# A ring of three PSUM banks for the first products of an expert layer, with two kinds of transposes sharing one bank

## The reference

```python
x = x + conv(_ln_c(x))            # attention over 256 positions, 8 images of 64 channels
t = _to_tokens(x)                 # 2048 tokens of 64 channels
t = t + ffn(_ln_t(t))
# ffn: the router picks 2 of 8 experts for each token, gates sum to 1
h1 = jnp.einsum('nc,ehc->neh', flat, w1)      # 64 -> 682
h3 = jnp.einsum('nc,ehc->neh', flat, w3)      # 64 -> 682
h = jax.nn.silu(h1) * h3
y = jnp.einsum('neh,ech->nec', h, w2)         # 682 -> 64
out = jnp.einsum('ne,nec->nc', gates, y)
```

## Time and profile before

| | |
|---|---|
| median of 3 runs | 235.94 us (235.25 to 236.06) |
| profiled execution, its own time | 233.65 us |
| its span | 231.9 us |
| mean granted TensorE clock | 0.826 of full speed |
| TensorE matmul busy | 156.4 us (67%) |
| TensorE weight load busy | 135.8 us (59%) |
| VectorE busy | 109.8 us (47%) |
| GpSimd busy | 85.7 us (37%) |
| ScalarE busy | 72.1 us (31%) |
| HBM traffic | 143 GB/s over the span |

### The profile page before, as it was taken

One profiled execution on the slowest core, in us unless ns is written; L12 is line 12 of the kernel. 1 busy time (PEld: TensorE's weight loads), 2 busy tenths in 40 slices (PEclk: granted clock), 3 DMA queues, 4 the chain that ended last, 5 costly groups with the idle time before them and its releaser, 6 DMA issues.

```text
span 231.9 us, 4952 instructions
## 1 busy us (share of the span) xinstructions
PE 156.4 (67%) x1714; PEld 135.8 (59%) x1714; DVE 109.8 (47%) x398; ACT 72.1 (31%) x154; POOL 85.7 (37%) x109
## 2 busy tenths in 40 slices
PE   2647898698924000049988888888888889898031
PEld 2527896687813000048977777777777777786010
DVE  2696598679457700014544444444444444442050
ACT  2236445341000000024533444444444444432011
POOL 6142520206777777600033333333333333336400
PEclk9999999655555555557999999999999999999655
DMA  4999600000101000020276766677677766500053
GB/s 136 429 390 420 285 0 3 0 0 7 31 18 33 23 29 23 29 47 15 91 269 219 252 231 236 224 240 246 222 233 233 244 220 201 168 11 20 23 181 91
DMA packets 16314, 33.47 MB, mean 144 GB/s; under 512 B 7826, under 2 KB 9010, under 8 KB 15778
## 3 DMA queue, kind: packets, MB, share of 16 engines
q1 hardware_dynamic: 14018, 30.80, 38.8%
q0 software_dynamic: 2272, 2.36, 3.1%
HBM read 25.94 MB, written 7.21 MB: 143 GB/s over the span
## 4 chain that ended last, share of the span: by engine, by line
issue 40%; POOL 29%; DVE 9%; PE 9%; DMA 5%; ACT 3%; POOLq 1%; SPq 0%; ACTq 0%
POOL ys L335 15%; POOL xs L294 13%; PE bank L803 2%; DVE xn L477 2%; PE bank L791 2%; DMA y_in<-ys 2%; DVE kq_right L509 1%; POOL rstd L278 1%; DVE neg_max L514 1%; DMA x_sb<-x_tok 1%; PE bank L769 1%; PE bank L753 1%; DMA xs<-rows,pos 1%; DMA ys<-y_out,y_row 1%; ACT probs L367 1%
## 5 line engine op out<-in xcount | busy, mean ns | idle before, releaser
L917 PE MATMUL bank<-x_cols,weights 64*128 64x128 f32 x468 | 64.2, 287 | 10.3 <-ACT act_sb L429 9.3
L713 DVE TENSOR_TENSOR hid<-bank,act_sb 128x512 f32<-128x512 f32 (+1 forms) x60 | 40.5, 676 | 62.2 <-ACT act_sb L429 60.5
L335 POOL DMA_INDIRECT ys<-y_out,y_row x39 | 37.3, 957 | 83.7 <-DVE y_out L721 77.1
L917 PEld LDWEIGHTS bank<-x_cols,weights 64*128 64x128 f32 x468 | 57.3, 194 | 17.1 <-ACT act_sb L429 12.3
L919 PE MATMUL bank<-x_cols,weights 64*128 64x128 f32 x468 | 64.2, 287 | 0.0
L919 PEld LDWEIGHTS bank<-x_cols,weights 64*128 64x128 f32 x468 | 57.3, 194 | 0.0
L429 ACT ACTIVATE act_sb<-bank 128x512 f32<-128x512 f32 (+1 forms) x60 | 35.1, 586 | 43.6 <-PE bank L917 43.5
L294 POOL DMA_INDIRECT xs<-rows,pos x32 | 31.6, 986 | 9.7 <-issue 9.7
L935 PE MATMUL bank<-hid,weights 128*64 128x128 f32 x468 | 30.6, 277 | 0.5 <-ACT y_cols L437 0.5
L935 PEld LDWEIGHTS bank<-hid,weights 128*64 128x64 f32 x468 | 25.8, 137 | 3.8 <-issue 2.3
L897 PE MATMUL bank<-ident,x_pairs 128*128 128x128 f32 x39 | 8.9, 309 | 27.1 <-DVE x_pairs L701 27.1
(11 more groups left out here) (123 smaller groups left out, 192.4 us busy)
## 6 DMA issues: line engine op xcount, KB each, us to landing
weights<-experts SPq DMA_DIRECT2D x39, 576.0 KB, 4.1
xs<-zeros SPq DMA_DIRECT2D x4, 1056.0 KB, 9.0
x_in<-xs SPq DMA_DIRECT2D x39, 33.0 KB
y_in<-ys SPq DMA_DIRECT2D x4, 256.0 KB, 3.7
ys<-y_out,y_row POOLq DMA_INDIRECT x39
xs<-rows,pos POOLq DMA_INDIRECT x32
out<-result SPq DMA_DIRECT2D x8, 64.0 KB, 2.1
x_sb<-x_tok SPq DMA_DIRECT2D x1, 384.0 KB, 3.7
```

The lines of the kernel that those rows point to most:

```text
L335: nc.gpsimd.indirect_dma_start(ys, bass.IndirectOffsetOnAxis(ap=y_row[:, HALVES * i + h:HALVES * i + h + 1], axis=0), y_out[:, i % RING, h ...
L713: nc.vector.tensor_tensor(live(i, hid[:, g % HRING, :]), live(i, H3_BANK[g % 3][:]), live(i, act_sb[:, g % 3, :]), ALU.mult).then_inc(hid_ ...
L917: first_ = nc.tensor.matmul(H1_BANK[g % 2][:, dst], weights[0:C, slot, at:at + P], x_cols[0:C, i % 2, src], start=True, stop=True)
```

## The change

`H1_BANK` becomes three banks. The bank for them comes from `X_BANK` and `R_BANK`, which now share one: the turned rows use its columns 0 to 255, the turned results columns 256 to 383.

- `up(g)` writes the H1 bank that group g-3 used, and waits for `silu(g - 3)` in place of `silu(g - 2)`. `silu(g)` reads `H1_BANK[g % 3]`.
- `turn_y(i - 2)` stands behind the three `down` groups of round i. It waits in addition for `x_cols_ready` of round i+2 as counted from its own number, which in the loop is `columns(i + 1)` of the current round: ScalarE must have read the turned rows from the shared bank.
- `turn_x(i)` waits in addition for `gate(i - 4)` from round 4 on, so that VectorE has read the turned results; the wait for `rank_read` moves from `turn_y(0)` to `turn_x(0)`.

```diff
-        H1_BANK, H3_BANK, Y_BANK, X_BANK, R_BANK = bank[0:2], bank[2:5], bank[5], bank[6], bank[7]
+        H1_BANK, H3_BANK, Y_BANK = bank[0:3], bank[3:6], bank[6]
+        X_BANK, R_BANK = bank[7][:, 0:PAIR], bank[7][:, PAIR:PAIR + P]
...
-                nc.scalar.activation(live(i, act_sb[:, g % 3, :]), live(i, H1_BANK[g % 2][:]), ACT.Silu
+                nc.scalar.activation(live(i, act_sb[:, g % 3, :]), live(i, H1_BANK[g % 3][:]), ACT.Silu
...
                 pe.wait_ge(x_paired, i + 1)
                 if i == 0:
                     pe.wait_ge(t_cols_ready, NBLK)
+                    pe.wait_ge(rank_read, NBLK)
                 else:
                     pe.wait_ge(x_cols_ready, i)
+                if i >= 4:
+                    pe.wait_ge(gated, i - 3)
...
-                if g >= 2:
-                    pe.wait_ge(silu_done, g - 1)
                 if g >= 3:
+                    pe.wait_ge(silu_done, g - 2)
                     pe.wait_ge(hid_done, g - 2)
...
-                        first_ = nc.tensor.matmul(H1_BANK[g % 2][:, dst], weights[0:C, slot, at:at + P],
+                        first_ = nc.tensor.matmul(H1_BANK[g % 3][:, dst], weights[0:C, slot, at:at + P],
...
                 pe.wait_ge(y_copied, i + 1)
                 if i >= 1:
                     pe.wait_ge(gated, i)
-                else:
-                    pe.wait_ge(rank_read, NBLK)
+                pe.wait_ge(x_cols_ready, min(i + 4, NT))
...
                 if i + 1 < NT:
                     turn_x(i + 1)
-                if 2 <= i < NT:
-                    turn_y(i - 2)
                 if 1 <= i <= NT:
                     for s in range(STEPS):
                         down(STEPS * (i - 1) + s)
-                if i >= NT:
+                if i >= 2:
                     turn_y(i - 2)
```

## The result

| | before | changed |
|---|---|---|
| median | 236.0 us (235.25 to 239.0) | 228.67 us (228.53 to 229.63) |
| profiled execution, its own time | 233.65 us | 228.53 us |
| its span | 231.9 us | 226.8 us |

The ratio is 0.971 (95% interval 0.967 to 0.975): faster by 7.3 us, not by 12.6. The 239.0 of the kernel before is a slow execution; the ratio compares fast ones alone. The profiled execution of before had been one of the short ones; against it the gain is 5.1 us.

A forecast was written before the change was run, and what follows sets the result against it. TensorE's rounds in the expert layer bound the kernel, with waits for `act_sb`. Gains of 13.1 and 0.1 us less 0.5 lost, rounded to 12.6, took the median from 235.94 to 223.4 us; range 221.5 to 230.5 us.

The forecast's parts named there:

- the likeliest case: The forecast itself: the third group no longer waits, expert layer rounds fall to 4.83 us, median 223.4 us; chance 0.60.
- Late reports, not a late array: Expert layer: TensorE's matmuls are on time; only the report of a finished group is late, now and then by 0.8 us.
- the chance of no change: Rival: TensorE's first two groups really end 0.8 us late, so the bank saves little; about 235 us; chance 0.13.
- The third bank's 13.1 us: Rounds 3 to 17: the third group stops waiting for a late `silu`, saving 0.87 us in each of 15 rounds.
- The transpose at its new place, costed at nothing: Result transpose behind the second products: it takes the same 0.20 us of TensorE at either place, so no cost.
- The columns' margin of a few tenths: Columns end 3.9 to 4.6 us into a round; the result transpose, starting at about 4.65, does not wait.
- the second case: Rival: late reports move onto the columns, the result transpose waits, rounds take 5.1 to 5.3 us; 227 to 230.5 us; chance 0.18.
- The sum: Whole kernel: 13.1 us from the third bank, 0.1 from rounds 1 and 2, less 0.5 at the end, rounded to 12.6.
- DMA hidden: Weight loads: DMA share rises to 0.81 of a 4.83 us round; loads land in 4.1 us, issued 9.7 us ahead.
- The end's 0.5 us: After round 19's second products: gate and scatter come later, and 0.5 us is taken as lost.

The follow-up runs named there:

- the run one `silu` later: Kernel before with the scatters put off until the second `silu` of the next round has ended; on chip 0 229.2 us, ratio 0.970.

## Why the prediction was right and wrong

The direction and the range held: 228.67 lies in 221.5 to 230.5. The point, 223.4, did not, and the likeliest case was the wrong one of the two.

- **Late reports, not a late array.** Right, and it is what put the chance of no change low. In the changed kernel the second `silu` is 1.5 us late while TensorE goes on with the third group, the turned rows and 24 second products on schedule, and reports that were due 0.90 us apart come 0.18 apart. The modelled ends that "Perfetto Trace Analysis" in the Trainium skill ("Tensor Engine Instruction (MATMUL, LD_WEIGHTS)") warns of are good here: on chips 9 and 12 every `silu` of rounds 1 to 18 starts 0.03 to 0.04 us behind them.
- **The third bank's 13.1 us.** Wrong in its cause. The step said that the bank lets the third group pass a late `silu`. Further down the same text said that the move would put the first report on time; with that, two banks are enough, and I did not draw this conclusion. The two-bank run on chip 0 shows it: 5.32 us against 5.32. Whether the bank without the move would have removed the wait there, as the step had it, was not run. The bank is worth 0.05 us a round where nothing is held (4.97 in round 2 of the changed kernel, 5.02 with two banks).
- **The transpose at its new place, costed at nothing.** Wrong: 0.15 us a round (5.02 against 4.87 on chip 9). What the transpose itself takes, 0.20 us from start to start, was read at its old place; behind the second products it adds 0.26 us to a round, at the old place 0.11 (round 1, without it, takes 4.76 or 4.71 us, round 2, with it, 4.87 before and 4.97 after). In 15 rounds that is 2.2 us; with the third bank's 0.05 the changed kernel pays 0.10 a round, 1.5 us.
- **The columns' margin of a few tenths.** Wrong, and the main miss. I put their end at 3.9 to 4.6 us of the round; it is 4.93. This is the second case, given 0.18: reports of the second group, the third and the turned rows held, and the columns late by it. Its number for the columns, 4.9, was right by luck, for the hold is another: I had the three released one by one, at 2.8, 3.65 and 4.5 us, and they come together, at 3.56, 3.74 and 3.83, after which `silu`, `silu`, columns in ScalarE's order do the rest. Rounds became 5.33 us where that case said 5.1, or 5.3 with a little more: 0.35 us above the 4.97 of round 2, which has no scatter, 5.3 us in 15.
- **The sum.** 15 x 0.87 became 15 x 0.38 in the first pair of profiles and 15 x 0.43 in the pair of chip 0 (5.75 and 5.32): 0.87 less 0.15 less 0.35. The 0.87 was measured against round 18, and that it has a full load was misread: it turns the rows of one slot only, and takes 4.76 us in the five traces without held reports that have the old order and a bank for each transpose, where the rounds before it take 4.87. In the kernel before it is itself held a little (4.83), so the slip is 0.04 us a round.
- **DMA hidden.** Right; the share is 0.73 to 0.79 in full rounds of 5.3 us, for the 0.81 estimated at 4.83; a load lands in 5.7 us for 4.1, and no first product waits for it.
- **The end's 0.5 us.** Round 19 to the last scatter grew by 0.51 us in the first pair, but shrank by 0.8 us on chip 0 (10.21 to 9.44). It stays a guess.
- **What no case had:** that the wait to be removed is there on one chip and not on another. Where reports are not held, the changed kernel has nothing to win. It was not run there itself; its two-bank variant is 1.1% slower there, and 0.05 us in each of 17 rounds less would leave about 1.3 us, an estimate from the two runs.

## What to carry to other kernels

When an engine starts late although the one it waits for has finished by the profile, look at what a third engine does at that moment before adding buffers: here a shift of the scatters by 0.7 us removed the wait, and the added bank did nothing. To tell a late report from late work, compare the distance between two reports with the work between them: a group that takes 0.9 us cannot have ended 0.2 us behind the one before it. A change of two parts should be run with each part alone, since the one that was meant to pay may not be the one that does. And a stall that is seen on one chip should be looked for on a second one before a kernel is rebuilt around it.

## What was not expected of the hardware

- In the first comparison and on chip 0 TensorE's reports came late in every round with scatters; in the traces of chips 9 and 12 never: 236 and 222 us for the kernel before, with rounds of 5.7 us and, by the other runs' profiles, 4.87. Rounds 1 and 2, which have no scatter, are on time in all traces. Each chip was used at one time only, so the chip and whatever else differed between these times (where the program's buffers lay, for one) are not told apart.
- The profile has a mark of it, outside the expert layer. The page gives no landing time for the first stage's scatters in the six traces with late reports, and 2.2 us in the eight without; here the kernel before, then the run with two banks on chip 9:

```profile
xs<-rows,pos POOLq DMA_INDIRECT x32
```

```profile
xs<-rows,pos POOLq DMA_INDIRECT x32, 2.2
```

- The mark comes from records of raised semaphores that are missing: of the 747 that the engines' own instructions should leave, 50 to 75 are not there in each of the six traces, and 0 to 10 in the others. Lost records and late reports go together. Whether the recording itself holds the reports no run tells: each execution here has its clock listed, so none seems to have been without it.
- Where reports are held, the hold moves with the scatters. Measured from the start of a round's first scatter, reports due up to 0.8 us after it are on time (0.13 us late at most). Most due at 1.2 to 3.0 us are late and come 2.7 to 3.2 us after it, close together. The exception is the first `silu`'s report in the kernel before: due at 1.2, it comes at 2.0 to 2.1, and in round 18 at 1.3. Reports due at 3.1 us or later are on time again. GpSimd's two issues themselves end at 2.2 us.
- The weight loads are not needed for it: in round 18 of the changed kernel the DMA share is 0.04, and the second group's report still comes 1.46 us late.
- Whether the issue of the scatter or its transfers cause the hold is open: the runs without scatters and with memsets in their place fell on chips without it. So is whether scatters behind the first `silu` would bring chip 0 from 5.75 to 4.87 us a round and 223 us; the run one `silu` later gave 5.14 us and 229.2 us there with two lines added to the kernel before, as much as the whole change.
